# One stage for the second layer's output projection, layer norm and routing

## The reference

```
x = x + einsum('bqhd,hdo->bqo', y, Wout)          # second attention's output projection
n = (x - mean(x)) / sqrt(var(x) + 1e-5)           # layer norm
scores = sigmoid(n @ gate_w.T)                    # 16 experts
inds = top_k(scores + expert_bias, 8)
gate = 2.826 * scores[inds] / sum(scores[inds])   # spread back over 16 columns
x = x + sum_e gate[e] * down_e(silu(gate_e(n)) * up_e(n)) + shared expert
```

## Time and profile before

| | us |
|---|---|
| median of 3 runs | 2119.53 |
| lowest and highest of them | 2110.45, 2119.8 |
| the profiled execution's own time | 2113.68 |
| its span in the profile | 2112.0 |
| busy in the span: PE, DVE, ACT, POOL | 1881.6, 1427.0, 1194.0, 636.3 |

### The profile page before, as it was taken

One profiled execution on the slowest core, in us unless ns is written; L12 is line 12 of the kernel. 1 busy time (PEld: TensorE's weight loads), 2 busy tenths in 40 slices (PEclk: granted clock), 3 DMA queues, 4 the chain that ended last, 5 costly groups with the idle time before them and its releaser, 6 DMA issues. The chain is left out here.

```text
span 2112.0 us, 40164 instructions
## 1 busy us (share of the span) xinstructions
PE 1881.6 (89%) x9926; PEld 1180.6 (56%) x9926; DVE 1427.0 (68%) x6195; ACT 1194.0 (57%) x2237; POOL 636.3 (30%) x964
## 2 busy tenths in 40 slices
PE   5899999999985829975899999999999994699998
...
DMA packets 107054, 210.86 MB, mean 100 GB/s; under 512 B 16524, under 2 KB 46234, under 8 KB 105408
## 3 DMA queue, kind: packets, MB, share of 16 engines
...
...
## 5 line engine op out<-in xcount | busy, mean ns | idle before, releaser
L679 DVE CUSTOM_DVE_ANT_0 a1ms<-a1S,mask_q 128x128 bf16<-128x128 f32 (+1 forms) x758 | 387.8, 553 | 173.2 <-issue 168.5
L736 ACT ACTIVATE a1work<-a1T 128x512 f32<-128x512 f32 x576 | 330.2, 597 | 297.3 <-PE a1T L838 296.8
L679 DVE CUSTOM_DVE_ANT_0 a0ms<-a0S,mask_q 128x384 bf16<-128x384 f32 (+2 forms) x752 | 379.8, 553 | 102.5 <-issue 93.3
L736 ACT ACTIVATE a0work<-a0T 128x512 f32<-128x512 f32 x576 | 329.9, 597 | 189.6 <-PE a0T L838 178.8
L817 PE MATMUL a1O<-a1work,a1v 128*33 128x512 f32 (+3 forms) x1536 | 304.2, 496 | 0.9 <-POOL a1work L647 0.9
L838 PE MATMUL a0T<-a0qT,a0kT 128*128 128x512 f32 (+3 forms) x768 | 265.9, 393 | 15.3 <-ACT a0work L736 5.1
L838 PE MATMUL a1T<-a1qT,a1kT 97*128 97x512 f32 (+3 forms) x768 | 263.4, 391 | 2.3 <-DMA a1qT<-a1mr 2.3
L777 PE MATMUL a0S<-a0kS,a0qS 128*128 128x384 f32 (+2 forms) x752 | 229.7, 361 | 19.0 <-PEq L305 8.0
L838 PEld LDWEIGHTS a1T<-a1qT,a1kT 97*128 97x128 f32 x768 | 131.7, 189 | 201.8 <-ACT a1work L736 144.4
L838 PEld LDWEIGHTS a0T<-a0qT,a0kT 128*128 128x128 f32 x768 | 131.7, 189 | 169.2 <-ACT a0work L736 125.8
L777 PE MATMUL a1S<-a1kS,a1qS 96*128 96x128 f32 (+1 forms) x758 | 219.9, 351 | 2.4 <-DVE a1held L676 1.7
...
## 6 DMA issues: line engine op xcount, KB each, us to landing
...
```

Of the source, the lines that this page charges most:

```text
L679: nc.vector.tensor_tensor_reduce(masked_s[spare][:, 0:c1 - c0], buf[:, 0:c1 - c0], k.mask_q[:, SEQ - w + c0:SEQ - w + c1], 1.0, NEVER, ALU ...
L736: nc.scalar.activation(prob_of(g, p)[:, h, :], t_ps[slot % 2][:, :], ACT.Exp, scale=scale)\
```

## The change

`project_out`, `ln_stats` and `route` of the second layer become one stage, `project_and_route`, written out without loops. The attention now writes its pairs of heads side by side (`rows_of_1`), so that PE transposes straight from `attn1` (`turn_heads`, three PSUM banks) and ACT's copies into `o1st` are gone. PE goes through 32 chunks, four for a supertile, and projects chunk m-2 after it has turned chunk m. DVE adds a supertile, takes its statistics, and makes mean and deviation of its 4 tiles (`variance`, with the root on ACT in `deviation`), then normalises them (`norm`). PE turns a normalised supertile one supertile later (`turn`) and multiplies by the router two later (`logits`). The rest `xl` moves from POOL to DVE (`make_xl`). The choice over 32 tiles (`gates`, called once with HT = TILES) has the same instructions as before. The gates are transposed in two groups of four supertiles. The expert weights are loaded into a freed part of `attn1` once half of the chunks are turned; the first weight is rounded before the last supertile's copies, the other two behind the exponential; POOL now makes two of the three rests. In `moe_1` most work tiles and the gate rows lie in `attn1` instead of tiles of their own; its instructions are the same.

```diff
...
+def project_and_route(k, attn, w_out, wr, bias, xh, xl, gate_rows, weights, sources):
...
+                def add(s):
+                    dve.wait_ge(y_done, NC * (s + 1))
+                    rows = k.x[:, s * TPS:(s + 1) * TPS, :]
+                    tt(rows, y_ps[s % 2][:, :].rearrange("p (t d) -> p t d", t=TPS), rows, ALU.add).then_inc(added, 1)
+                    dve.wait_ge(added, s + 1)
+                    link(*[nc.vector.bn_stats(k.stats[:, t, :], k.x[:, t, :]) for t in range(s * TPS, (s + 1) * TPS)])
+                def variance(s):
+                    rows = slice(s * TPS, (s + 1) * TPS)
+                    mean_e, m2_e, mean_o, m2_o = (k.stats[:, rows, i] for i in (1, 2, 4, 5))
+                    mean, rstd, dev = k.mean[:, rows], k.rstd[:, rows], k.tmp[:, rows]
+                    link(tt(mean, mean_e, mean_o, ALU.add), tt(dev, mean_e, mean_o, ALU.subtract), tt(rstd, m2_e, m2_o, ALU.add))
+                    signal(ts(mean, mean, 0.5, None, ALU.mult))
+                    link(tt(dev, dev, dev, ALU.mult))
+                    signal(nc.vector.scalar_tensor_tensor(rstd, dev, D / 4.0, rstd, ALU.mult, ALU.add))
+                    at["variance", s] = count[0]
+                def make_xl(s):
+                    dve.wait_ge(kept, 2 * s + 2)
+                    cols = slice(s * ST, (s + 1) * ST)
+                    tt(xl[:, cols], xs[s % 2][:, :], xh[:, cols].bitcast(F32), ALU.subtract).then_inc(xl_ready, 1)
+                def norm(s):
+                    rows = slice(s * TPS, (s + 1) * TPS)
+                    dve.wait_ge(std_ready, s + 1)
+                    link(nc.vector.reciprocal(k.rstd[:, rows], k.rstd[:, rows]))
+                    if s >= 2:
+                        dve.wait_ge(xT_done, s - 1)
+                    for t in range(TPS):
+                        last = normalise_tile(k, xn[s % 2][:, t, :], s * TPS + t)
+                    last.then_inc(xn_ready, 1)
...
+                for s in range(NST):
+                    add(s)
+                    variance(s)
+                    if s:
+                        make_xl(s - 1)
+                    norm(s)
+                dve.wait_ge(*k.routers_loaded)
+                make_xl(NST - 1)
+                gates(0)
+                w_hi, w_lo = weights[2]
+                dve.wait_ge(w_split, 3)
+                tt(w_lo, raws[2], w_hi.bitcast(F32), ALU.subtract)
...
+                sp.wait_ge(turned, NC * 2 * BATCHES_BELOW)
+                for raw, source in zip(raws, sources):
...
+                def turn_heads(m):
+                    s, n = divmod(m, NC)
+                    if m >= BANKS:
+                        pe.wait_ge(aT_ready, m - BANKS + 1)
                     for t in range(TPS):
+                        last = nc.tensor.transpose(aT_ps[m % BANKS][:, t * P:(t + 1) * P], attn[:, s // 2 * NC + n, s % 2 * TPS + t, :],
+                                                   k.ident[:, :])
+                    last.then_inc(turned, 1)
+                def project(m):
+                    s, n = divmod(m, NC)
+                    pe.wait_ge(aT_ready, m + 1)
+                    if n == 0 and s >= 2:
+                        pe.wait_ge(added, s - 1)
+                    for t in range(TPS):
+                        last = nc.tensor.matmul(y_ps[s % 2][:, t * D:(t + 1) * D], aT[m % RING][:, t * P:(t + 1) * P], w_out[:, n, :],
+                                                start=n == 0 and t == 0, stop=n == NC - 1 and t == TPS - 1)
+                    last.then_inc(y_done, 1)
+                def turn(s):
+                    pe.wait_ge(xn_ready, s + 1)
+                    if s:
+                        pe.wait_ge(kept, 2 * s)
+                    for t in range(TPS):
+                        last = nc.tensor.transpose(xT_ps[:, t * P:(t + 1) * P], xn[s % 2][:, t, :], k.ident[:, :])
                     last.then_inc(xT_done, 1)
+                def logits(s):
+                    pe.wait_ge(kept, 2 * s + 1)
+                    if s:
+                        pe.wait_ge(lg_ready, s)
                     for t in range(TPS):
+                        last = nc.tensor.matmul(l_ps[:, t * E:(t + 1) * E], xs[s % 2][:, t * P:(t + 1) * P], wr[:, :],
                                                 start=True, stop=True)
                     last.then_inc(l_done, 1)
...
+                pe.wait_ge(*k.routers_loaded)
+                for m in range(CHUNKS + AHEAD):
+                    if m < CHUNKS:
+                        turn_heads(m)
+                    if m >= AHEAD:
+                        project(m - AHEAD)
+                    s, n = divmod(m - AHEAD, NC)
+                    if n == NC - 1:
+                        if s >= 1:
+                            turn(s - 1)
+                        if s >= 2:
+                            logits(s - 2)
+                logits(NST - 2)
+                turn(NST - 1)
+                logits(NST - 1)
+                turn_gates(0)
+                turn_gates(1)
...
+                def keep_heads(m):
+                    act.wait_ge(turned, m + 1)
+                    if m >= RING:
+                        act.wait_ge(y_done, m - RING + 1)
+                    nc.scalar.copy(aT[m % RING][:, :], aT_ps[m % BANKS][:, :]).then_inc(aT_ready, 1)
+                def deviation(s):
+                    act.wait_ge(chain, at["variance", s])
+                    rows = k.rstd[:, s * TPS:(s + 1) * TPS]
+                    nc.scalar.activation(rows, rows, ACT.Sqrt, scale=1.0 / D, bias=k.eps[:, :]).then_inc(std_ready, 1)
+                def keep(s):
+                    act.wait_ge(xT_done, s + 1)
+                    if s >= 2:
+                        act.wait_ge(l_done, s - 1)
+                        act.wait_ge(xl_ready, s - 1)
+                    nc.scalar.copy(xs[s % 2][:, :], xT_ps[:, :]).then_inc(kept, 1)
+                    nc.scalar.copy(xh[:, s * ST:(s + 1) * ST], xT_ps[:, :]).then_inc(kept, 1)
+                def keep_logits(s):
+                    act.wait_ge(l_done, s + 1)
+                    nc.scalar.copy(lg[:, s * TPS:(s + 1) * TPS, :], l_ps[:, 0:TPS * E].rearrange("p (t e) -> p t e", t=TPS))\
+                        .then_inc(lg_ready, 1)
+                def exponentials(half):
+                    tiles = slice(half * HT, (half + 1) * HT)
+                    act.wait_ge(lg_ready, NST)
+                    nc.scalar.activation(pr[:, tiles, :], lg[:, tiles, :], ACT.Exp, scale=-1.0).then_inc(pr_ready, 1)
+                def round_weight(n):
+                    nc.scalar.copy(weights[n][0], raws[n]).then_inc(w_split, 1)
...
+                for m in range(CHUNKS + 4):
+                    if m < CHUNKS:
+                        keep_heads(m)
+                    s, n = divmod(m, NC)
+                    if n == 1 and s >= 2:
+                        keep(s - 2)
+                    if n == 2 and s >= 3:
+                        keep_logits(s - 3)
+                    if n == 3 and s >= 1:
+                        deviation(s - 1)
                 act.wait_ge(weights_loaded, 16 * len(weights))
+                round_weight(0)
+                keep(NST - 1)
+                keep_logits(NST - 2)
+                keep_logits(NST - 1)
+                exponentials(0)
+                round_weight(1)
+                round_weight(2)
                 for s in range(NST):
...
-                for u in rounds(pool, NST // 2):
-                    for par in range(2):
-                        pool.wait_ge(xh_ready, lin((u, par), 1, 1))
-                        cols = bass.ds(lin((u, par), ST, 0), ST)
-                        nc.gpsimd.tensor_tensor(xl[:, cols], xs[par][:, :], xh[:, cols].bitcast(F32), ALU.subtract)\
-                            .then_inc(xl_ready, 1)
...
-        act_g = [sb(f"s{i}", [P, ST], F32) for i in range(2)]
+        spare = iter([room[:, :, :, :].rearrange("p g t c -> p (g t c)")[:, n * ST:(n + 1) * ST] for n in range(P // 4)])
+        act_g = [next(spare) for _ in range(2)]
         QUARTER = E // 4
-        gb = [sb(f"gb{i}", [P, QUARTER, ST], F32) for i in range(4)]
-        ones = sb("one", [P, ST], F32)
-        prod = [sb(f"pr{i}", [P, ST], F32) for i in range(2)]
-        h = [sb(f"h{i}", [P, ST], F32) for i in range(2)]
+        prod, h, y = ([next(spare) for _ in range(2)] for _ in range(3))
+        ones = next(spare)
+        rows = room[:, 8:16, :, :].rearrange("p g t c -> p (g t c)")
+        gb = [rows[:, q * QUARTER * ST:(q + 1) * QUARTER * ST].rearrange("p (e n) -> p e n", n=ST) for q in range(4)]
         hh = [sb(f"hh{i}", [P, ST], F32R) for i in range(HBUF)]
         hl = [sb(f"hl{i}", [P, ST], F32R) for i in range(HBUF)]
-        y = [sb(f"y{i}", [P, ST], F32) for i in range(2)]
...
-            project_out(k, "o1", attn, a_v, 8)
-
-        with ExitStack() as c:
+                attention(k, "a1", 2, 32, 64.0 ** -0.5, rows, rows_of_1, work, rest, wait_stored(stores))
```

(10 more changed lines are left out.)

184 lines of the change are left out of this document (82 added, 102 removed).

## The result

The changed kernel took **2101.26 us** (median of 4 runs, 2099.72 to 2102.94) where the kernel before, beside it, took 2117.35 us (4 runs, 2110.45 to 2119.80). The ratio is 0.9929, with a 95% interval of 0.9903 to 0.9956: the change made the kernel faster, by 16.1 us of the medians, somewhere between 9 and 21. 2104 was forecast, within 2096 to 2114. The profiled execution has a span of 2100.9 us, 11.1 less than before.

A forecast was written before the change was run, and what follows sets the result against it. TensorE was taken to bound the projection and the half-clock pass, then DVE's choice chain, then SP's 32 stores. Gain 12.8 less 0.7 gave 12.1 us; 2115.9 less 12.1 gave 2103.8, predicted 2104, range 2096 to 2114.5.

The forecast's parts named there:

- Begin.: Start of the merged stage: TensorE starts at 1699.65 instead of 1701.79, 2.1 us earlier, as transposes read `attn1` itself.
- Projection with the pass in it: Merged stage at full clock: 42.8 us of projection plus 6.6 of pass, last add at 1749.5 where it was 1746.04.
- DVE's path: Each supertile, last product to last normalised tile: 5.6 us, asked for after 6.6, so DVE keeps up with 1.0 margin.
- a late DVE: Rival in the merged stage: DVE's supertile path 1.6 us longer, gain 8; chance 0.21 together with collision and gaps.
- Tail: From the last add to the start of the choice of experts: 12.2 us, the choice at 1761.7 instead of 1774.53.
- Choice and gates: Choice unchanged, gain 0; first four gate transposes signalled together, 0.7 us of loss; SP's stores stay at 14.72 us.
- Attention and experts: Stages around the merged one: 0 taken for both; 0.1 us more on each POOL multiply would cost 12.8 us.
- the collision of the last normalisation with GpSimd: Rival in the tail: last normalise meets POOL's first subtraction, loses up to 4.8 us, gain 7; chance 0.21 with late DVE, gaps.
- the forecast's case: The whole change gains 10 to 14.5 us; chance 0.60.
- the merged stage would drag the clock down: Rival in the merged stage: the pass's work halves TensorE's clock, a loss of 37 us, time 2153; chance 0.05.
- The gaps at 64 waits: Rival in the merged stage: 0.1 us lost at each chunk wait, gain 6, time 2110; chance 0.21 with late DVE, collision.

The follow-up runs named there:

- Experiment 1: The kernel before, with the second attention's heads written side by side and transposed straight from `attn1`, without ACT's 32 copies: 2108.68 us.
- Experiment 4: The changed kernel with turns and logits of all supertiles behind the projection's last product: 2110.45 us, ratio to before 0.9989; run again with two ACT orders mended.
- 3: The kernel before, with 24 unread identity products ahead of the normalising pass and 3 more in each of its rounds: 2106.83 us.
- 4b: The changed kernel with turns and logits behind the projection, first xT copy ahead of the last root, first weight rounding behind the exponentials: 2102.53 us, ratio 0.9933.

## Why the prediction was right

By its own steps, in its order:

- *Begin.* 1.1 us of rest predicted, 1.03 measured, and no fall of the clock. Experiment 1 gives this part 3.7 us up to the last add; the prediction's sum had 3.4 (see there).
- *Projection with the pass in it.* Last add 49.85 us after TensorE's start predicted, 1752.27 - 1702.24 = 50.03 measured; adds 6.60 apart for 6.6. Experiment 4 shows the 7.2 us directly.
- *DVE's path.* 5.6 us predicted from a supertile's last product to its last normalised tile. Measured are 5.2 from the add, and with the prediction's 0.15 ahead of it some 5.35; the margin was 1.2 us for 1.0. No run made this path longer, so what a late DVE would have cost was not measured.
- *Tail.* This is the term that was mis-sized: 12.2 us from the last add to the choice predicted, 1763.15 - 1752.27 = 10.9 measured. The first normalisation came at +3.1 for +4.0, in three parts of 0.3 each. The statistics ended at +1.6 and not +1.9: their four instructions took 1.08 us in the loop of before and 0.87 written out. The chain behind them took 0.8 us for 1.1, since I took the prices of the 32-column instructions as they stood. Root, `make_xl(6)` and reciprocal took 0.7 for 1.0. Another 0.4 us lay behind the first normalisation, most of it in the last logits: 1.9 us from their start to the start of their copy for 2.15, of which the prediction works out 8 x 0.22 = 1.76 and gives no row for the rest. For the small instructions a margin was named, for the other two not.
- *Choice and gates.* DVE's 18.1 us for 18.0; the first store 1.38 us after the transposes began and not 0.74, a loss of 0.64 where 0.7 stood; stores 14.70 for 14.72.
- *End of the stage.* The prediction has no term here. From the end of SP's stores to the experts' first product it is 1.54 us, and was 1.88 before. No run shows why.
- *Attention and experts.* 0 predicted. The multiplies average 1477 ns for 1478, and the stage is 302.0 us for 302.1. The attention ended 2.65 us later in this one execution, which lies within the 8 us over which that point moved among the executions of this study.

Sum: 12.1 predicted, 13.6 in D. Of the 1.5 between, 1.3 are the tail's and 0.3 the stage's end; the other differences are below 0.2 each and nearly cancel. The time itself, 2101.26 for 2104, is no closer proof: the medians lie 16.1 apart, the 2.5 beyond D stand in no stage, and they are within the interval.

What the rivals foresaw: the collision of the last normalisation with GpSimd missed by 0.48 us, as the prediction's own "some 0.5" had it. Nothing in the kernel keeps the two apart, so that the forecast's case came and not this one, priced at up to 4.8 us, hung on half a microsecond. That the merged stage would drag the clock down was not the case. The reason given, that products stand between the groups, fits 3, where products kept among the same work went with 1.00; since no run has the pass alone without waits, it is not shown against the other reason, that the merged stage leaves TensorE no wait. The gaps at 64 waits did not come: TensorE is busy 19.00 of 19.00 us.

From 111.3 the runs make a ladder: direct heads to 107.4; norms by supertile inside the projection, the pass behind it, to 102.8 (4b); the pass inside to 97.7. The middle step also holds the moves off GpSimd and the stage boundaries, which no run took apart.
